# Loading and splitting an expert layer's weights one stage earlier

## What is computed

```python
x = x + _L0_gnn_ref(layernorm(x), ...)   # attention over 100000 edges
x = x + _L0_ffn_ref(layernorm(x), ...)   # 32 experts, the best one each
x = x + _L1_gnn_ref(layernorm(x), edge_index, weight, attn_l, attn_r)
x = x + _L1_ffn_ref(layernorm(x), Wr, br, ln_g, ln_b, W1, b1, W2, b2)

# _L1_gnn_ref: only the first n edges count
xt = (x @ weight).reshape(-1, 4, 64)
alpha = softmax(leaky_relu(alpha_l + alpha_r, 0.01), axis=1)
tmp = einsum('nh,nhd->nd', alpha[:n], xt[col[:n]])   # gathered rows

# _L1_ffn_ref: 8 experts, 256 -> 1024 -> 256, the best two of each node
h = gelu(einsum('end,edh->enh', xe, W1) + b1)
y = einsum('enh,ehd->end', h, W2) + b2
out = (weights * sel).sum(axis=1)
```

## Time and profile before

| | us |
|---|---|
| median of 3 runs | 3399.04 (3393.04 to 3404.69) |
| profiled execution, its own time | 3405.51 |
| its span, first to last instruction | 3403.9 |
| TensorE busy | 2192.1 (64%) |
| VectorE busy | 1809.5 (53%) |
| GpSimd busy | 1500.0 (44%) |
| ScalarE busy | 1275.6 (37%) |

### The profile page before, as it was taken

The page is one execution under the profiler, slowest core; times in us unless marked ns, Lnnn a source line. Parts: engine busy times, 40 slices in busy tenths (PEclk is TensorE's granted clock), DMA queues, the critical chain, the costliest instruction groups (busy, mean ns, idle before and its releaser), DMA issues. The chain is left out here.

```text
span 3403.9 us, 51773 instructions
## 1 busy us (share of the span) xinstructions
PE 2192.1 (64%) x13091; PEld 1853.0 (54%) x13092; DVE 1809.5 (53%) x4075; ACT 1275.6 (37%) x2808; POOL 1500.0 (44%) x1568
## 2 busy tenths in 40 slices
PE   2999966777777777776280753505200999999920
PEld 2888865565566556564170642304200899999920
DVE  4111026777777677775845344267534555555543
ACT  0444445555566565554020431302003434433310
POOL 1056137777777777774405343272370000000056
PEclk7999977888888888887655886855555999999965
DMA  6356356666655555556331442223126111111146
GB/s 135 128 206 239 162 214 203 204 204 204 209 161 144 146 144 144 142 140 76 91 96 68 145 148 69 71 50 90 44 102 226 44 47 49 49 49 44 48 140 170
DMA packets 244173, 429.47 MB, mean 126 GB/s; under 512 B 59464, under 2 KB 168707, under 8 KB 237374
## 3 DMA queue, kind: packets, MB, share of 16 engines
q0 software_dynamic: 73824, 206.40, 22.8%
q1 hardware_dynamic: 144274, 208.69, 18.4%
q10 hardware_dynamic: 25948, 12.88, 1.5%
HBM read 266.36 MB, written 161.85 MB: 126 GB/s over the span
## 5 line engine op out<-in xcount | busy, mean ns | idle before, releaser
L715 POOL DMA_INDIRECT sum_ring<-h_tab,gnn_edge_row x880 | 840.8, 956 | 268.3 <-issue 260.4
L976 PE MATMUL sum_bank<-sum_ring,sum_one_hot 128*128 128x264 f32 x1760 | 580.7, 493 | 225.8 <-issue 202.2
L976 PEld LDWEIGHTS sum_bank<-sum_ring,sum_one_hot 128*128 128x128 f32 x1760 | 417.8, 247 | 343.6 <-issue 231.7
L641 PE MATMUL rows_bank<-rows_w_rows,rows_xnT 128*128 128x264 f32 x1568 | 359.5, 388 | 1.8 <-ACT rows_xnT L263 1.8
L641 PEld LDWEIGHTS rows_bank<-rows_w_rows,rows_xnT 128*128 128x128 f32 x1568 | 295.7, 191 | 50.6 <-ACT rows_xnT L263 2.2
L1777 POOL DMA_DIRECT2D moe_tile<-sorted x58 | 42.1, 725 | 626.4 <-PE moe_bank L1885 603.8
L765 ACT ACTIVATE sum_distance_by_lane<-all_iota,gnn_minus_local 128x128 bf16<-128x128 f32 x880 | 267.4, 386 | 0.1
L831 DVE TENSOR_TENSOR sum_ring<-sum_ring,sum_bank 128x1024 f32<-128x1024 f32 x220 | 265.7, 1209 | 0.5 <-ACT sum_ring L779 0.4
L965 PEld LDWEIGHTS sum_bank<-gnn_dst_half,sum_one_hot_T 128*128 128x128 f32 x1760 | 224.2, 203 | 40.8 <-issue 37.3
L965 PE MATMUL sum_bank<-gnn_dst_half,sum_one_hot_T 128*128 x1760 | 228.4, 287 | 26.4 <-ACT sum_one_hot_T L758 14.3
L1905 PE MATMUL moe_bank<-moe_w_high,moe_hidden_low 128*128 x896 | 244.2, 273 | 0.0
(11 more groups left out here) (398 smaller groups left out, 4109.1 us busy)
## 6 DMA issues: line engine op xcount, KB each, us to landing
h_tab<-rows_h_rows SPq DMA_DIRECT2D x49, 1056.0 KB, 3.9
sum_local_rows<-local_tab SPq DMA_DIRECT2D x110, 256.0 KB, 3.8
sorted<-sum_zero SPq DMA_DIRECT2D x49, 384.0 KB
moe_stage<-in_L_ffn_W_dram SPq DMA_DIRECT2D x16, 1024.0 KB, 5.6
moe_tile<-sorted POOLq DMA_DIRECT2D x58, 256.0 KB, 3.6
results<-moe_y SPq DMA_DIRECT2D x56, 256.0 KB
sum_ring<-h_tab,gnn_edge_row POOLq DMA_INDIRECT x880, 3.7
sorted<-sum_zero SPq DMA_DIRECT2D x49, 256.0 KB
```

The costliest lines, as they stand in the source:

```text
L641: last = nc.tensor.matmul(bank[2 + r % 4][:, 0:W0], norm.xT[:, u, c * P:(c + 1) * P], wx[:, c, r, :], start=(c == 0), stop=(c == DC - 1))
L715: nc.gpsimd.indirect_dma_start(ring[:, t % (RING * ST), :], None, k.h_tab, bass.IndirectOffsetOnAxis(k.edge_row[:, t:t + 1], 0)).then_inc( ...
L976: last = nc.tensor.matmul(sum_b[j][:, 0:W0], hot[:, m % 2, t, :], ring[:, m % RING * ST + t, :], start=(u == 0), stop=(u == G - 1))
```

## The change

The weights of `experts1` move into a class `Weights`, whose memory is taken at the far end before `attend1` begins. A piece is loaded in two transfers of 512 KB in place of one of 1 MB, and the pieces of W2 are cut otherwise (half the rows of two experts). Pieces 0 to 11 are loaded and split inside the product half of `attend1`, one for every four tiles: the loops of ScalarE, VectorE and SyncE over the tiles are written out for that. Pieces 12 to 14 are loaded by SyncE in `route1` behind the store of `x`. Piece 15 is loaded in `experts1`, where pieces 12 to 15 are split on ScalarE behind the first two `turn`s and on VectorE behind the first two `split_x`. TensorE waits for 8 pieces ahead of the first tile, and for all 16 ahead of its loop.

```diff
+class Weights:
+    def load(self, sp, n):
+        if n >= 3:
+            sp.wait_ge(self.low_ok, n - 2)
+        _, to, src = self.part(n, self.stage[:, n % 3, :])
+        if n < E1:
+            for c in range(DC):
+                sp.dma_start(to[:, c], src[:, c]).then_inc(self.staged[n % 3], 16)
+        else:
+            for i in range(2):
+                sp.dma_start(to[:, :, i * D:(i + 1) * D], src[i]).then_inc(self.staged[n % 3], 16)
+    def high(self, act, n):
+        to, src, _ = self.part(n, self.stage[:, n % 3, :])
+        act.wait_ge(self.staged[n % 3], 32 * (n // 3 + 1))
+        self.nc.scalar.activation(to[0], src, ACT.Copy, scale=WS).then_inc(self.high_ok, 1)
+    def low(self, v, n):
+        to, src, _ = self.part(n, self.stage[:, n % 3, :])
+        v.wait_ge(self.high_ok, n + 1)
+        self.nc.vector.scalar_tensor_tensor(to[1], src, WS, to[0], ALU.mult, ALU.subtract).then_inc(self.low_ok, 1)
+PIECES, EARLY = 2 * E1, E1 + E1 // 2
...
 def attend1(nc, a, k):
...
-            tiles(sp, NT, 2, save)
+            for n in range(3):
+                k.weights.load(sp, n)
+            for t in range(NT):
+                save(t, t % 2)
+                if t % 4 == 3 and t // 4 + 3 < EARLY:
+                    k.weights.load(sp, t // 4 + 3)
             stored.all(sp, NT)
...
             norm.keep(act, 0, 0, xt_ps)
-            with act.Fori(0, (NT - 1) // 2) as i:
-                for u in range(2):
-                    norm.keep(act, i * 2 + u + 1, 1 - u, xt_ps)
-                    emit(i, u)
+            for t in range(NT - 1):
+                norm.keep(act, t + 1, (t + 1) % 2, xt_ps)
+                emit(t // 2, t % 2)
+                if t % 4 == 2:
+                    k.weights.high(act, t // 4)
             emit((NT - 1) // 2, 0)
...
-            tiles(v, NT, 2, lambda t, u: norm.normalise(v, t, u))
+            for t in range(NT):
+                norm.normalise(v, t, t % 2)
+                if t % 4 == 3:
+                    k.weights.low(v, t // 4)
...
 def route1(nc, a, k):
...
             sp.dma_start(k.x3.rearrange("(t p) f -> p t f", p=P), k.x[:, :, :]).then_inc(saved, 16)
+            for n in range(EARLY, EARLY + 3):
+                k.weights.load(sp, n)
             sp.wait_ge(saved, 16)
...
 def experts1(nc, a, k):
...
-            for n in range(PIECES):
-                low_ok.slot(sp, n)
-                _, m, src = part(n)
-                sp.dma_start(stage[:, n % 3, :].rearrange("p (c h) -> p c h", c=m), src).then_inc(staged[n % 3], 16)
+            for n in range(EARLY + 3, PIECES):
+                k.weights.load(sp, n)
...
             turn(0, 0, e[0])
             turn(1, 1, e[1])
+            for n in range(EARLY, PIECES):
+                k.weights.high(act, n)
             gelu(0, 0, e[0])
...
             split_x(0, 0)
             split_x(1, 1)
+            for n in range(EARLY, PIECES):
+                k.weights.low(v, n)
             split_h(0, 0)
...
-            low_ok.done(pe, PIECES - 1)
+            pe.wait_ge(k.weights.low_ok, E1)
             e = registers(nc, PE, route.expert[0:1, 0:2], E1 - 1)
             turn(0, 0)
             turn(0, 1)
             up(0, 0, e[0])
+            pe.wait_ge(k.weights.low_ok, PIECES)
             with pe.Fori(0, T1 // 2) as i:
```

More of the change, by code:

```diff
@@ L114, in __exit__, with sb @@
             self.nc.all_engine_barrier()
-    def sb(self, name, shape, dt=F32):
-        return self.ctx.enter_context(self.nc.sbuf_tensor(f"{self.name}_{name}", shape, dt))
+    def sb(self, name, shape, dt=F32, side="left"):
+        return self.ctx.enter_context(self.nc.sbuf_tensor(f"{self.name}_{name}", shape, dt, side=side))
     def banks(self, n=8):
@@ L1431, in _, with __init__, rest, part @@
                     nc.tensor.matmul(bank[2 * u + 1][:, 0:D], hT[:, u, :], col(w2, e[u]), start=True, stop=True).then_inc(y_ps.sem, 1)
+class Weights:
+    def __init__(self, nc, s, a):
+        self.nc, self.a = nc, a
+        self.w1 = [s.sb(f"w1_{n}", [P, DC, E1 * F1], F16, "right") for n in ("high", "low")]
+        self.w2 = [[s.sb(f"w2_{n}0", [P, MC // 2, E1 * D], F16, "right")] for n in ("high", "low")]
+        self.stage = s.sb("stage", [P, 3, 2048], F32, "right")
+        self.staged = [s.sem(f"staged{u}") for u in range(3)]
+        self.high_ok, self.low_ok = s.sem("high_ready"), s.sem("low_ready")
+    def rest(self, s):
+        for t, n in zip(self.w2, ("high", "low")):
+            t.append(s.sb(f"w2_{n}1", [P, MC // 2, E1 * D], F16))
+    def part(self, n, staged):
+        if n < E1:
+            to = [t[:, :, n * F1:(n + 1) * F1] for t in self.w1]
+            return to, staged.rearrange("p (c h) -> p c h", c=DC), self.a["L1_ffn_W1"][n].rearrange("(c p) h -> p c h", p=P)
+        j, e = (n - E1) // (E1 // 2), (n - E1) % (E1 // 2) * 2
+        to = [t[j][:, :, e * D:(e + 2) * D] for t in self.w2 if j < len(t)]
+        return (to, staged.rearrange("p (c h) -> p c h", c=MC // 2),
+                [self.a["L1_ffn_W2"][e + i, j * F1 // 2:(j + 1) * F1 // 2, :].rearrange("(c p) h -> p c h", p=P) for i in range(2)])
+    def load(self, sp, n):
+        if n >= 3:
+            sp.wait_ge(self.low_ok, n - 2)
+        _, to, src = self.part(n, self.stage[:, n % 3, :])
+        if n < E1:
+            for c in range(DC):
[12 more added lines that the diff above has]
+PIECES, EARLY = 2 * E1, E1 + E1 // 2
 def attend1(nc, a, k):
@@ L1722, in experts1 @@
         route, DVE, PE, SC = k.route1, mybir.EngineType.DVE, mybir.EngineType.PE, mybir.EngineType.Activation
-        w1 = [s.sb(f"w1_{n}", [P, DC, E1 * F1], F16) for n in ("high", "low")]
-        w2 = [s.sb(f"w2_{n}", [P, MC, E1 * D], F16) for n in ("high", "low")]
-        stage = s.sb("stage", [P, 3, 2048])
+        k.weights.rest(s)
+        w1, w2 = k.weights.w1, k.weights.w2
         lg, lb, b1 = s.sb("gain_T", [P, DC, E1]), s.sb("shift_T", [P, DC, E1]), s.sb("b1_T", [P, E1, MC])
@@ L1734, in experts1 @@
         small, small_ps, small_ok = s.sem("small_loaded"), s.sem("small_in_psum"), s.sem("small_ready")
-        staged = [s.sem(f"staged{u}") for u in range(3)]
-        high_ok, low_ok = Count(s, "high_ready", 3), Count(s, "low_ready", 3)
         tile_in, out_ok = [s.sem(f"tile_loaded{u}") for u in range(2)], Landed(s, "y_written", 2)
@@ L1742, in experts1 @@
         xhi_ok, hhi_ok = Count(s, "x_high", 2), Count(s, "hidden_high", Q)
-        PIECES = 2 * E1
         block = s.block()
[L1747 to L1752, removed]
         @block.sync
@@ L1781, in _ @@
         def _(act):
[L1782 to L1786, removed]
             act.wait_ge(small_ok, 1)
@@ L1818, in _ @@
         def _(v):
-            low_ok.start(v)
             v.wait_ge(small, 64)
@@ L1824, in _ @@
             nc.vector.tensor_copy(b1[:, :, :], bank[7][:, 4 * E1:4 * E1 + E1 * MC].rearrange("p (e m) -> p e m", e=E1)).then_inc(small_ok, 1)
[L1825 to L1828, removed]
             for n in (xs_ok, xhi_ok, hs_ok, hhi_ok, y_ok):
@@ L1904, in down @@
                         for n, (pw, ph) in enumerate(passes):
-                            last = nc.tensor.matmul(bank[6 + u][:, h * D:(h + 1) * D], hh[ph][:, u, m, h * P:(h + 1) * P], w2[pw][:, m, bass.ds(e * D, D)],
+                            last = nc.tensor.matmul(bank[6 + u][:, h * D:(h + 1) * D], hh[ph][:, u, m, h * P:(h + 1) * P], w2[pw][m // (MC // 2)][:, m % (MC // 2), bass.ds(e * D, D)],
                                                     start=(m == 0 and n == 0), stop=(m == MC - 1 and n == 2))
                 last.then_inc(y_ps.sem, 1)
-            low_ok.done(pe, PIECES - 1)
+            pe.wait_ge(k.weights.low_ok, E1)
             e = registers(nc, PE, route.expert[0:1, 0:2], E1 - 1)
@@ L2048, in build @@
                 return store(nc, a, k)
+            early = Stage(nc, "moe1_early")
+            k.weights = Weights(nc, early, a)
             attend1(nc, a, k)
-            if stop == 3:
-                return store(nc, a, k)
             route1(nc, a, k)
         experts1(nc, a, k)
+        early.ctx.close()
         combine1(nc, a, k)
```

## The result

The change makes the kernel slower: 3471.2 us (median of 4 runs) against 3401.9, ratio 1.0214 (95% interval 1.0186 to 1.0243), 69 us. The direction was forecast; the size was not: 3441 was predicted, and 3462 was the upper end of the range. The profiled execution has a span of 3469.4 us against 3403.9, 65.5 us more.

A forecast was written before the change was run, and what follows sets the result against it. No single engine bounds the kernel; the bound changes by stage. The opening's -42 us and the graph layer's +84 us summed to +42, taking the median from 3399.0 to 3441 us, range 3405 to 3462.

The forecast's parts named there:

- The opening's gain: Last expert stage's opening: TensorE no longer waits for the pieces ahead of its first tile; 42 us gained, bounds 38 to 46.
- TensorE's new idle: Last stage's opening: a new idle of about 6 us behind the first `up`, waiting for piece 15.
- The split in series with TensorE: Product half: queue order leaves TensorE idle 5.2 us at each of 12 pieces; graph layer costs 84 us in all.
- 0.1 us of address arithmetic a tile: Product half: loops written out save this ahead of the stores over 49 tiles, up to 5 us, in the lower end only.
- The clock: Product half: after each gap, the first two tiles of each four take 2.11 us, the rest 1.11.
- the rival of the low clock throughout: Product half: low clock and slow stores throughout, +102 - 42 = +60 us, 3459; chance 0.14.
- The load ahead of the store: Product half: a load queued before a store moves the emit from 7.7 to 8.6, 0.9 us a cycle, 8 us in all.
- The range: Whole kernel: 3405 to 3462 us, from the ends of the unknowns, +7 to +64.
- The rival of the slack: Product half: idle time of ScalarE and VectorE absorbs the split if VectorE normalises the next tile first; 3357 us, chance 0.06.

The follow-up runs named there:

- no_loads: The changed kernel without the nine loads of pieces 3 to 11 in the product half; 3436.0 us against 3410.1 before, ratio 1.0071.
- low_later_no_loads: The changed kernel with VectorE's low part two tiles later and the nine product-half loads left out; 3375.3 us against 3398.8 before, ratio 0.9924.

## Why the prediction was wrong

- **The opening's gain: right.** -42 us forecast, -41 measured. Piece 15 was issued, landed and was split as worked out (5.3 us to landing, 5.2 taken), TensorE's new idle is 7.75 us where 6 were forecast.
- **The split in series with TensorE: right in mechanism, somewhat high in size.** A cycle without a load was put at 12.9 us; without loads they average 12.2 (first to last high part, 2116.51 and 2250.56 in no_loads). The split cost 67 us, 5.5 a piece, for 76 by the prediction's 6.3. A part of it is that the loops written out save more than they were priced at: from the start of emit to the issue of the l_tab store 1.1 us pass before and 0.8 after (2104.23 to 2105.02). The prediction's 0.1 us of address arithmetic a tile, and the fetching of straight code set against it, no run shows.
- **The clock: right.** It was low behind the gap and came back within the four tiles (0.56 from 2115 to 2116, then 1.00), and two of the four went at about 2.0 us. No run takes it away; by the prediction's own sum (emit at 7.7 for 6.2) it is worth up to 1.5 us a cycle, an estimate, since the store that ends the cycle is issued behind tiles at the low clock. So the rival of the low clock throughout, whose 3459 lies nearest to what was measured, isn't what happened.
- **The load ahead of the store: wrong, and this made the miss.** The step was "Ahead of the store it lands at about 3.9 + 4.7 = 8.6", so 0.9 us over 7.7 for a cycle with a load. Measured it is 4.9 us (44.5 over nine), and the emit came 11.8 us behind transpose 4 (2112.12 to 2123.93), where in no_loads a cycle has 7.3 (2145.36 to 2152.69). Nine times 4.0 is 36 us; less the 9 us that the series was put too high, that is the 27 us between 84 and 111. Counted from transpose 4, in the cycle shown: the load is issued at 3.5, its bulk moves from 6.5 to 9.1, in 2.6 us as forecast, the stores' data to 10.2, and the first store is home at 11.8. Two things were left out: the 3 us from issue to movement, and that the store's data and its landing come behind the load's. I had let both land together. In the cycles with a piece of W2 the load moves sooner and slower, and the sum is the same. Why a load starts late or moves slowly no run shows.
- **The range: wrong at the top.** Its upper end varied the clock and the landing, took 9.9 for this step, and never let the store's time follow the load's. With the load's median landing of 5.6 and the store's 2.1 in sum the step is 3.9 + 5.6 + 2.1 = 11.6 and the forecast 9 x 10.2 + 3 x 6.3 - 42 = +69. This is worked out after the event, and that it meets the measured 69 is partly luck, since the series in it is still too high.
- **The rival of the slack: refuted as the kernel stands, right with another order.** low_later_no_loads shows all but 16 us of the split hidden, once the next tiles are normalised ahead of the low part, which is the condition that the rival named.

## What to carry to other kernels

Idle shares say that work may fit, the written order of each queue says whether it does: follow one moved instruction through every in-order queue until the loop closes. Where a bulk load is issued ahead of a small store whose landing frees a buffer, add up its delay to movement, its transfer and the store's own landing (here the emit came 11.8 us behind the first transpose, and 7.3 without a load). Put it where no store is due; here that took moving the load's one line to the tile ahead of the split, and gave back 43 us. Where work is moved into a loop, price the loop's shortest round trip and not its busy time.

## What the runs showed that was not expected

- A load of 1 MB (two transfers of 512 KB) that was issued at 2115.58 moved 64 KB from 2116.5 to 2117.1, then nothing until 2118.6, and then the rest at about 380 GB/s. The load at 2201.02, in packets of 1 KB, moved steadily at about 200 GB/s.
- From another issuing engine such a load still cost 2.8 of 4.8 us, though issued 1.2 us earlier, counted from the emit, and so ahead of one tile's stores more.
- A GpSimd indirect transfer of 0.97 us took 1.88 to 2.55 us in each of the twelve cases in which it began while VectorE ran a two-input instruction of 2.28 us over fast memory.
